# A fused cross-attention and FFN kernel: rows scaled one by one, tiles quantised one by one, unit 0 of the weights first

## What is computed

```
x = x + tanh(g_xattn) * matmul(fake_quant(layernorm(x)), fake_quant(ctx))
x = x + tanh(g_ffn)   * ffn(layernorm(x))

def fake_quant(x, s, z): return (clip(round(x / s + z), 0, 255) - z) * s

def ffn(x):                                    # SELECT = 128, blocks of 16 along a row
    A, g = quant_act(x)                        # g = max(max|x| / (448 * 6), 1e-8), over ALL rows
    gate, up = A @ Wg.T * g, A @ Wu.T * g      # Wg, Wu, Wd: int4 per block of 16
    Am, gm = quant_act(silu(gate) * up)
    return Am @ Wd.T * gm
# quant_act: x / g, each block of 16 rounded to fp8 (e4m3) with the scale
#   max(max|block| / 448, 1e-8); the last 128 columns get a second fp8 term of what is left
```

## Time and profile before

| | us |
|---|---|
| median of 3 runs (818.03 to 818.71) | 818.54 |
| the profiled execution, its own time | 818.77 |
| its span, from the first to the last instruction | 817.0 |
| PE busy in the span | 731.0 |
| first product of the FFN starts (PE L1276) | 139.68 |
| the 16th product of the opening is done (ACT's last `silu_open`, waiting for it, starts at 216.23) | 216.1 |

### The profile page before, as it was taken

The page is one execution under the profiler, slowest core; times in us unless marked ns, Lnnn a source line. Parts: engine busy times, 40 slices in busy tenths (PEclk is TensorE's granted clock), DMA queues, the critical chain, the costliest instruction groups (busy, mean ns, idle before and its releaser), DMA issues.

```text
span 817.0 us, 10350 instructions
## 1 busy us (share of the span) xinstructions
PE 731.0 (89%) x3473; PEld 334.5 (41%) x3473; DVE 556.3 (68%) x957; ACT 311.3 (38%) x382; POOL 343.7 (42%) x206
## 2 busy tenths in 40 slices
PE   0599003999999999999999999999999999999998
PEld 0144002545444444444444444444444444444443
DVE  5459789894475756675757575745898888988800
ACT  2798972445252524343434343430222122121100
POOL 1536766769374747584848575740000000000000
PEclk9989655999999999999999999999999999999999
DMA  8910598339588897979697969774265654555320
GB/s 308 353 60 14 166 279 147 80 64 190 145 173 212 187 211 174 223 169 227 145 232 163 231 163 236 157 157 164 49 152 162 182 129 149 132 161 121 88 60 26
DMA packets 228884, 131.56 MB, mean 161 GB/s; under 512 B 201712, under 2 KB 212976, under 8 KB 227824
## 3 DMA queue, kind: packets, MB, share of 16 engines
q1 hardware_dynamic: 228848, 131.12, 65.2%
HBM read 61.88 MB, written 19.66 MB: 100 GB/s over the span
## 4 chain that ended last, share of the span: by engine, by line
PE 78%; DVE 5%; POOL 5%; DMA 5%; ACT 3%; SPq 2%; issue 1%; DVEq 0%
PE acc L1276 47%; PE acc L1330 27%; DMA big<-in_ctx_dram 3%; PE acc L1223 2%; POOL big L739 1%; POOL h_in L734 1%; DVE big L1535 1%; ACT wbuf_all L919 1%; POOL wbuf_all L715 1%; POOL wbuf_all L708 1%; POOL big L728 1%; DMA wbuf_all<-in_L_ffn_w_up_dram 1%; SPq L455 1%; DMA mid<-big 1%; DMA x_d<-big 1%
## 5 line engine op out<-in xcount | busy, mean ns | idle before, releaser
L1276 PE MATMUL acc<-mid 128*128 128x512 f16 x1920 | 415.1, 379 | 0.0
L1276 PEld LDWEIGHTS acc<-mid 128*128 128x128 f16 x1920 | 187.9, 98 | 226.1
L1330 PE MATMUL acc<-big,mid 128*128 128x512 f16 x1040 | 224.6, 379 | 0.0
L818 POOL TENSOR_TENSOR h_in<-wbuf_all,h_in 128x1024 f16<-128x1024 f32 (+1 forms) x56 | 114.4, 2044 | 97.2 <-ACT h_in L1115 97.1
L1330 PEld LDWEIGHTS acc<-big,mid 128*128 128x128 f16 x1040 | 101.8, 98 | 122.7
L708 POOL TENSOR_TENSOR wbuf_all<-wbuf_all,w_inv 128x1024 f32<-128x1024 f32 (+1 forms) x67 | 125.2, 1873 | 43.6 <-DVE w_inv L1448 43.6
L1558 DVE SCALAR_TENSOR_TENSOR h_out<-acc,gs,silu 128x256 f32<-128x256 f32 (+1 forms) x88 | 41.5, 471 | 102.6 <-ACT silu L956 65.3
L1442 DVE TENSOR_REDUCE tb<-wbuf_all 128x64 f32<-128x1024 f32 (+1 forms) x67 | 78.9, 1178 | 47.3 <-DMA wbuf_all<-in_L_ffn_w_gate_dram 22.2
L912 ACT ACTIVATE wbuf_all<-wbuf_all 128x1024 f32<-128x1024 f32 (+1 forms) x67 | 68.1, 1016 | 82.2 <-POOL wbuf_all L708 81.4
L1115 ACT ACTIVATE h_in<-wbuf_all 128x1024 f16<-128x1024 f32 (+1 forms) x56 | 56.9, 1016 | 103.1 <-DVE wbuf_all L1454 103.1
L1454 DVE SCALAR_TENSOR_TENSOR wbuf_all<-wbuf_all,tb 128x1024 f32<-128x1024 f32 (+1 forms) x56 | 65.1, 1163 | 0.3 <-issue 0.2
(11 more groups left out here) (159 smaller groups left out, 555.0 us busy)
## 6 DMA issues: line engine op xcount, KB each, us to landing
h_in<-h_d SPq DMA_DIRECT2D x8, 1376.0 KB, 7.0
wbuf_all<-in_L_ffn_w_gate_dram SPq DMA_DIRECT2D x21, 512.0 KB, 4.3
wbuf_all<-in_L_ffn_w_up_dram SPq DMA_DIRECT2D x21, 512.0 KB, 4.3
h_d<-h_out SPq DMA_DIRECT2D x80, 128.0 KB, 3.5
big<-in_ctx_dram SPq DMA_DIRECT2D x16, 512.0 KB, 10.7
wbuf_all<-in_L_ffn_w_down_dram SPq DMA_DIRECT2D x16, 512.0 KB, 4.5
big<-in_x_dram SPq DMA_DIRECT2D x8, 512.0 KB, 6.9
x_d<-big SPq DMA_DIRECT2D x8, 512.0 KB, 4.8
```

The source lines that it names most:

```text
L818: last = pool.tensor_tensor(nat[s % 4][:, H:H + cols], wbuf[:, s % 4, 0:cols], nat[s % 4][:, 0:cols], ALU.subtract)
L1276: last = pe.matmul(acc[m % 4][:, 0:cols], left[:, k, s * P:(s + 1) * P], w[:, right, k, 0:cols], start=(k == 0 and left is a_hi and right ...
L1330: last = pe.matmul(acc[2 * i + hf][:], left[:, k - ks.start, :], right[:, k, hf * MW:(hf + 1) * MW], start=(k == 0 and left is hi and righ ...
```

## The change

- A is no longer scaled by one g for all rows. Each row is scaled by itself: the layernorm multiplies by 2 x 1024 instead of 2, `coef_a(t)` takes a row's own maximum for the lower bound of its block scales, and the scale of silu and of h is a constant (`H_DOWN`). `gmx`, `gs`, `a_coef`, the spread by PE and all that waits on them are gone. Tile t can be quantised once tile t is normalised.
- `start_a` runs on POOL for all eight tiles. The power of two for rounding is made by one ACT pass (`magic_a`, Abs) where DVE L1524 and ACT `floor_a` made it. `fold_outliers` (12 DVE steps) is `fold_begin` (5), `magic_fold` (ACT) and `fold_end` (4); its scratch `mgo_a` moves from PSUM to SBUF.
- The pieces of unit 0 come first (0 to 3), then P (4 to 6). OPENING starts U0 P0 P1 U1 U2 U3.
- Of the 11 pieces of the opening, six (1, 4, 5, 8, 9, 10) are rounded back by `back_w`, one DVE instruction, in place of `whole_w` (ACT) and `back_open` (POOL); the others stay.
- x1 is stored without the row term; ACT adds it at the end (`base(t)`, between the halves of the last phase), and `finish(t)` waits for that.
- The normalisation of x1 is in groups of 2, 4 and 2 tiles (before 4 and 4). `quantise_x` of tiles 3, 4 and 5 is on ACT.
- `aT` and the transposed A (`a_t`) are laid out tile after tile, so that one transpose writes one contiguous stretch.
- SP's, POOL's, ACT's, DVE's and PE's lists are written in another order throughout the opening; loads of ctx stand between those of x; DVE's first step for the loop's first piece (`front(PIECE_LOOP)`) stands behind the last `h_open`; PE waits for all eight x1 before its 14 transposes.

```diff
-OPENING = tuple((kind, t) for q in range(NT // 2) for kind in "PU" for t in (2 * q, 2 * q + 1))
+OPENING = (("U", 0), ("P", 0), ("P", 1), ("U", 1), ("U", 2), ("U", 3), ("P", 2), ("P", 3),
+           ("P", 4), ("U", 4), ("U", 5), ("P", 5), ("U", 6), ("P", 6), ("P", 7), ("U", 7))
+POOL_BACK = (0, 2, 3, 6, 7,)
-        a_both = mid[:, 0:8192].bitcast(F16).rearrange("p (q r) -> p q r", q=2 * KT)
+        a_t = mid[:, 0:8192].bitcast(F16).rearrange("p (t v k r) -> p t v k r", t=NT, v=2, k=KT)
...
+            def magic_a(t):
+                act.wait_ge(a_started[t], 1)
...
+                    act.activation(tb[hf][:], xn_all[:, t, hf * MW:(hf + 1) * MW], ACT.Abs, scale=V_ABS).then_inc(a_magic, 1)
...
+            def base(t):
+                i = t % 2
+                act.wait_ge(x1_loaded[i], 16 * (t // 2 + 1))
+                act.activation(x1_t[:, i, :], x1_t[:, i, :], ACT.Identity, bias=row_term[:, t:t + 1]).then_inc(x1_based, 1)
...
-            for n in range(P_PIECES):
-                pe.wait_ge(piece_turned[buf(n)], 16)
+            pe.wait_ge(x1_ready, NT)
             pe.wait_ge(nat_a_lo, 1)
...
+            def coef_a(t):
+                dve.wait_ge(max_done, t + 1)
+                step(dve.tensor_reduce(a_top[:, t:t + 1], bmx[:, t, :], AX_X, ALU.max))
+                step(dve.tensor_scalar(a_low[:, t:t + 1], a_top[:, t:t + 1], TINY / GDIV, A_UP * TINY * TINY, ALU.mult, ALU.max))
+                step(dve.tensor_scalar(a_scale[:, t, :], bmx[:, t, :], 1.0 / FP8_MAX, a_low[:, t:t + 1], ALU.mult, ALU.max))
+                dve.reciprocal(bmx[:, t, :], a_scale[:, t, :]).then_inc(coef_ready, 1)
...
+            def fold_end(t):
+                dve.wait_ge(fold_magic, t // 2 + 1)
+                small, mg = (a.rearrange("p t n -> p (t n)") for a in (ro_h[:, :, :], mgo_a))
+                step(dve.scalar_tensor_tensor(out=small, in0=mg, scalar=MAGIC_FLOOR, in1=small, op0=ALU.max, op1=ALU.add))
+                step(dve.scalar_tensor_tensor(out=small, in0=mg, scalar=MAGIC_FLOOR, in1=small, op0=ALU.max, op1=ALU.subtract))
+                step(dve.tensor_tensor(blocks(mg), blocks(small), spread(omx_a[:, 1, :]), ALU.mult))
...
+            def back_w(n):
+                b = buf(n)
+                dve.wait_ge(w_rounded, n + 1)
+                w = blocks(wbuf[:, b, :])
+                dve.scalar_tensor_tensor(out=w, in0=w, scalar=MAGIC, in1=spread(w_max[:, b, :]), op0=ALU.subtract, op1=ALU.mult)\
+                    .then_inc(w_back[b], 1)
```

896 lines of the change are left out of this document (450 added, 446 removed).

## The result

| | before | after |
|---|---|---|
| median, us | 818.62 (818.03 to 818.71, 4 runs) | 804.83 (804.44 to 805.37, 4 runs) |
| the profiled execution / its span | 818.77 / 817.0 | 804.9 / 803.1 |
| first product of the FFN starts | 139.68 | 121.28 |
| the last product of the opening is done | 216.1 | 202.4 |

The account below looks back on a forecast made before the run. The first product's start, plus PE's losses in the opening's 16 products, was taken as the bound. Start 122.5 + 73 + 2 + 5.1 = 202.6, 13.5 us earlier than 216.1, gave 805 us for the median; range 796 to 816.

Parts of the forecast that it names:

- What bounds the kernel: Whole kernel: time is the first product's start, plus PE's losses in the opening's 16 products, plus an unchanged rest.
- The start of the weights: Opening: POOL's first `scale` starts at 57.4 instead of 63.92, bounds 63.9 and 54; first `attend` at 34.5.
- the one on the loads: First loads: early scalars and ctx between tiles of x bring the first `attend` forward, of which 5.5 us stay.
- The stretch to `lo_a(0)`: POOL's first `scale` to `lo_a(0)`: 41.5 us of passes and 18 idle, ending at 117.5 instead of 135.3.
- Rival (1): DVE's SBUF-only steps wait for POOL passes: 25 steps, 1.93 us each, opening ends at 229, time 832; chance 0.10.
- The start of PE: First product: starts at 122.5 instead of 139.68, behind `make_x1(7)`'s 14 transposes (122.2) and tile 0's transpose (121.8).
- The contiguous target: Transpose of tile 0: one contiguous target may shorten it, to between 3.5 and 4.3 us.
- The 16 products: Opening's products: 73 us plus 2 for the clock and 5.1 of waits, ending at 202.6 instead of 216.1.
- The term for P: Before the first product of 384 columns: P ready at about 130.5, U0 done at 129.7, so 0.8 us waiting.
- The clock: First matmuls of the opening: the granted clock climbing back from its low level costs 2 us.
- Tile 2: Opening, at U2: tile 2 late by 1 us, one of the waits totalling 5.5 us.
- At no cost: `base(t)` in the last phase, the loop's later first piece and contiguous A were costed at nothing.

Follow-up runs that it names:

- e4: Kernel after, with `lo_a(0)` ahead of `start_pool(2)` on POOL and the last two `make_x1` ahead of three DVE calls: 805.85 us.
- e1: Kernel after, with the scratch of the fold (`mgo_a`) back in PSUM: 803.23 us.
- e5: Kernel of e1, with block maxima of `max_a` and `coef_a`, and layernorm variance and root of tiles 2 to 5, also in PSUM: 799.21 us.
- e9: Kernel after, with piece 4 rounded back by `whole_w(4)` on ACT and `back_open(4)` on POOL instead of `back_w(4)` on DVE: 803.44 us.
- e12: Kernel after, with the first loads (x, scalars, ctx) in the order of the kernel before: 805.34 us.
- e8: Kernel before, with a constant in place of the maximum over all rows, list order kept: 817.58 us beside 817.27 for the kernel before.
- e11: Kernel after, with the transposed A laid out as before and `base(t)` left out: 804.35 us.
- e7: Kernel after, with `root(4)` (Sqrt) ahead of the first Silu and DVE's `spread_x1(4)` behind `coef_a(4)`, saving two table loads: 805.50 us.

## Where the prediction was right and where not

**What bounds the kernel.** Right that nothing counts behind the opening: the opening's end moved by 13.7 us (216.1 to 202.4), the time by 13.8. Half right that the time is the start of the first product plus a fixed rest. e4 moved the start by 2.4 us and nothing came of it; e1, e5 and e9 moved the start and the late tiles together, and all or most of it stayed (1.6, 5.6 and 1.4 us in the medians for 2.45, 5.1 and 1.44 at the start). The end has three limits (first product, pieces of P, tile 6), and they lay close to each other.

**The start of the weights.** The step that failed is the one on the loads. I had ctx between the tiles of x and the early scalars bring 5.5 us; e12 shows 0. The first `attend` came at 37.06 instead of 34.5, held 3.39 us by a flag of DVE, and POOL's first `scale` at 59.43 instead of 57.4. A gain of 4.5 us was there (2.8 against the profile of e8), from something else that I did not name.

**The stretch to `lo_a(0)`.** The end was right (117.5; measured 116.78), but by terms that cancelled, which is luck: POOL's first `scale` came 2.0 us late, its passes took 43.2 us instead of 41.5, and it was idle for 14.2 us instead of 18. The engine to count was not POOL. For most of its gaps I named a step of DVE or of ACT, but took them as gaps of POOL's list and didn't see that DVE had no gap at all (busy 97%). Of the 14 us, 4.4 were ended by a number of DVE and 9.6 by ACT, which waited for DVE in its turn: in e9, with `back_w(4)` off DVE, one such gap fell from 2.25 to 0.26 us. In e1 a relief of DVE by 2.9 us brought the start 2.0 forward, and in e9 POOL could take a pass more and the start still came earlier. Where two engines hand each other work, the one to count is the one with no idle time in the stretch to come, and the rows before gave the hint: DVE 59.91, POOL 48.32 of 71.37 us.

**The port.** Rival (1) had the mechanism and the wrong size. I took 0.7 us for each of the 25 steps, the rival 1.4 at the turning point. Summed over the rows after (each against its length beside an idle POOL), the steps waited some 13 us between 60 and 118 us and some 11 behind it; 11 over the 25 steps that the rival speaks of is 0.45 each. So it did not make the kernel slower than before, but it cost much: e5, which takes the port away from a part of these steps, is 5.6 us faster than the kernel after by the medians (4.5 by the ratios, 6.5 by the profiles). Short steps in a row beside a busy POOL are the worst case, since a pass of 1.9 us comes between each two: the layernorm's at 92.30 us in the kernel after took 1.88, 1.86 and 1.64 us instead of 0.16. The rival had every operation with SBUF on all sides wait; reductions and reciprocals of that kind did not.

**The start of PE.** Predicted 122.5, measured 121.28. The 14 transposes behind `make_x1(7)` and the DMA transpose of tile 0 were reckoned to end within 1 us of each other (122.2 and 121.8), and so they did (121.3 and 121.1). The contiguous target did not shorten the transpose (e11), 4.3 us as in the earlier trace rows, the upper end of my bounds.

**The 16 products.** Predicted 7.1 us over the 73 (5.1 waits, 2 clock; the text ahead of the sum has 5.5 for the waits, and DVE's items there add up to 65, not 64), measured 81.09 - 73 = 8.1: stops of 4.33 and 0.45, and the clock. The term for P was mis-sized: 0.8 us expected, 4.33 measured. The pieces were ready on POOL at 124.7, where I had 125.6, but the two transposes go one behind the other with `load_piece(9)` between, the second issued at 126.03, 3.39 us in the issue, landed at 131.6, so that P started at 131.72 instead of 130.5. And PE was through with U0 at 127.4 instead of 129.7, which is the larger part of the 3.5 us. The clock cost 3.2 us and not 2.0 (6.10 for 24 matmuls that take 5.2 at full clock, 10.28 for 48 that take 8.0), because behind the stop at P it was down a second time (0.77 in the mean of 131.72 to 142.0). Tile 2 was not late at all, tile 6 by 0.45. Together that is 1 us more than reckoned, and the start was 1.2 us early; the two cancel.

**At no cost.** `base(t)`, the layout and the two more table loads cost nothing that can be measured (e11, e7). The first unit of the loop had no stop.
